# Gathers of the second cross attention: ten at a group's beginning, six behind its first three items

## The reference, cut to what matters

```python
x = x + L0_ffn(layernorm(x))      # 64 experts, 8 of them per row
x = x + L1_xattn(layernorm(x), ctx_1024)
...
# end of L0_ffn: eight expert outputs of a row, weighted and added
slot_out = yb[dest] * topk_w
out = zeros(T, h).at[slot_token].add(slot_out)
...
# L1_xattn: 16 heads of 128; queries and keys are RMS-normalized over the head
q = rmsnorm(q, gq); k = rmsnorm(k, gk)
attn = softmax(einsum('bqhd,bkhd->bhqk', q, k) / sqrt(128))
out = einsum('bhqk,bkhd->bqhd', attn, v) @ Wo
```

## Time and profile before

| | |
|---|---|
| runs | 2551.67, 2556.38, 2558.78 us; median 2556.38 |
| profiled execution | 2556.95 us, span 2554.9 us |
| PE busy | 2466.8 us, 97% of the span |
| DVE, ACT, POOL busy | 1304.8, 1310.7, 753.5 us |
| mean granted TensorE clock | 0.989 of full speed |
| second cross attention in the span | from about 1258 to about 1883 us |

### The profile page before, as it was taken

How to read it: one execution, slowest core, us unless ns; L and a number is a source line. 1 busy time by engine, 2 the same in 40 slices (tenths; PEclk the granted TensorE clock), 3 DMA queues, 4 the chain that set the end, 5 groups by cost and what they waited for, 6 DMA issues and landing times. The chain is left out here.

```text
span 2554.9 us, 61096 instructions
## 1 busy us (share of the span) xinstructions
PE 2466.8 (97%) x19044; PEld 1873.8 (73%) x19044; DVE 1304.8 (51%) x4749; ACT 1310.7 (51%) x4901; POOL 753.5 (29%) x897
## 2 busy tenths in 40 slices
PE   8999999999999999999889999999989999999988
PEld 6888888877644444544567887788878888888877
DVE  4555555556577764444455444555434444444434
ACT  3555555554366666666576556666623333333342
POOL 1222222337546540001443333331151111111032
PEclk9999999999899999999999999999999999999999
DMA  6222222110140004441454444442372000000033
GB/s 208 65 66 66 66 66 66 57 56 1 47 165 13 1 18 120 125 122 42 102 158 118 114 117 111 125 124 88 88 178 89 8 8 8 8 8 7 10 96 122
DMA packets 176868, 195.20 MB, mean 76 GB/s; under 512 B 40074, under 2 KB 142536, under 8 KB 175971
## 3 DMA queue, kind: packets, MB, share of 16 engines
q1 hardware_dynamic: 153074, 157.81, 21.2%
q0 software_dynamic: 17744, 32.60, 5.6%
q10 hardware_dynamic: 5920, 3.28, 0.7%
HBM read 150.44 MB, written 56.62 MB: 81 GB/s over the span
## 5 line engine op out<-in xcount | busy, mean ns | idle before, releaser
L299 PE MATMUL rt_kn_key_ps<-moe_w_wk,all_big 128*128 128x512 f32 x560 | 250.2, 600 | 0.8 <-DVE moe_kn_stats L348 0.4
L858 ACT ACTIVATE xa_probsT<-xa_probsT_ps 128x256 f32<-128x256 f32 x512 | 190.8, 374 | 97.6 <-PE xa_probsT_ps L692 90.7
L2449 PEld LDWEIGHTS sa_work_ps<-sa_xnT,all_big 128*128 128x128 f32 x2048 | 230.0, 192 | 9.6 <-issue 6.2
L2449 PE MATMUL sa_work_ps<-sa_xnT,all_big 128*128 128x128 f32 x2048 | 233.5, 276 | 2.8 <-POOL all_big L2304 2.3
L715 PE MATMUL xa_misc_ps<-cross_folded,xa_mixT 128*128 128x256 f32 x1024 | 230.1, 380 | 0.0
L715 PEld LDWEIGHTS xa_misc_ps<-cross_folded,xa_mixT 128*128 128x128 f32 x1024 | 194.1, 190 | 28.9 <-issue 2.9
L692 PE MATMUL xa_probsT_ps<-all_ident,xa_probs 128*128 128x128 f32 x1024 | 197.4, 275 | 7.4 <-DVE xa_probs L999 6.7
L999 DVE TENSOR_SCALAR xa_probs<-xa_probs,xa_share 128x257 f32<-128x257 f32 x512 | 187.3, 387 | 14.3 <-DVE xa_share L997 0.5
L299 PEld LDWEIGHTS rt_kn_key_ps<-moe_w_wk,all_big 128*128 128x128 f32 x560 | 104.8, 192 | 120.6 <-issue 114.5
L850 ACT ACTIVATE xa_probs<-xa_probs,xa_shift,xa_row_scale 128x257 f32<-128x257 f32 x256 | 152.6, 596 | 78.7 <-DVE xa_shift L983 78.4
L320 ACT ACTIVATE rt_kn_key_ps<-rt_kn_key_ps 128x128 f32<-128x128 f32 x560 | 148.4, 265 | 85.0 <-PE rt_kn_key_ps L299 85.0
(11 more groups left out here) (402 smaller groups left out, 5022.5 us busy)
## 6 DMA issues: line engine op xcount, KB each, us to landing
all_big<-rk SPq DMA_DIRECT2D x256, 128.5 KB
xa_pair<-pairs SPq DMA_DIRECT2D x64, 256.5 KB, 14.5
pairs<-all_big SPq DMA_DIRECT2D x64, 128.5 KB, 3.1
moe_w_wk<-in_ctx_dram SPq DMA_DIRECT2D x64, 128.0 KB, 2.5
pairs<-xa_keys SPq DMA_DIRECT2D x64, 128.0 KB, 2.1
cross_folded<-in_L_ffn_w_gate_dram SPq DMA_DIRECT2D x32, 192.0 KB, 2.6
cross_folded<-in_L_ffn_w_up_dram SPq DMA_DIRECT2D x32, 192.0 KB, 2.8
ff_rows<-pairs SPq DMA_DIRECT2D x35, 128.0 KB, 2.1
```

The source lines that it names most:

```text
L299: pe.matmul(self.key_ps[m % self.banks][0:n, :], self.ctxT[:, c * P:c * P + n], self.wk[:, q * 512:(q + 1) * 512], start=True, stop=True). ...
L858: act.activation(probsT[:, b % 2, :, r * P:(r + 1) * P], probsT_ps[s % 2][:, 0:KB * P].rearrange("p (k n) -> p k n", k=KB), ACT.Copy).then ...
L2449: ins = pe.matmul(ps[:, j, :], w[:, c, h * HD:(h + 1) * HD], xnT[:, c, :], start=(c == 0), stop=(c == NC - 1))
```

## The change

`FRONT` is NB // 2 + 1 = 5. At b = 0 POOL now issues the gathers 0 to 9 in one go, and behind each of the first three mixed items (b = 1, 2, 3) two more, 10 to 15. Behind b = 4 to 7 it waits for nothing and gathers nothing. `norm_scale` keeps its place at b = 5, and the wait for all gathers keeps its place behind the list. Rows, counts and data of the gathers are the same.

```diff
         PORTION = G * K0 // NB
+        FRONT = NB // 2 + 1
...
                     if more and b == 0:
                         next_places(i + 2)
-                    if more:
-                        if b:
-                            pool.wait_ge(mixed, i * NB + (RING + b))
-                            apart(pool, pool_passed)
-                        gather(range(b * PORTION, (b + 1) * PORTION))
+                    if more and b == 0:
+                        gather(range(FRONT * PORTION))
+                    elif more and b <= NB - FRONT:
+                        pool.wait_ge(mixed, i * NB + (RING + b))
+                        apart(pool, pool_passed)
+                        gather(range((FRONT + b - 1) * PORTION, (FRONT + b) * PORTION))
```

## The result

The changed kernel takes 2585.07 us (median of four, 2582.83 to 2587.14) against 2556.47 us for the kernel before on the same chip: ratio 1.0114, 95% interval [1.0097, 1.0132], 29 us slower. The forecast was no change. The profiled span grew from 2554.9 to 2580.7 us, by 25.8.

The account below looks back on a forecast made before the run. PE was taken as the bound, busy 97% of the span, with gathers touching only seven stalls. Terms -2.4 + 1.5 + 1.3 = +0.4 us on the profiled execution gave a median of 2556.8 us, no change; range 2550.5 to 2562.

Parts of the forecast that it names:

- What bounds the kernel, and which load is late: Second cross attention, groups 0 to 5: PE waits for `weigh`, DVE 10.4 us for key scales; item 7's scales are late.
- Groups 1 to 5, what the front costs: Start of each group: front gathers delay item 4's keys and so item 5's scales; 0.3 us per group, 1.5 us.
- the price that it took for a gather in a burst: Delay of loads per front gather, from windows before group 0 with loads at about 108 GB/s: 0.29 us.
- six gathers: Groups 1 to 5: the front gathers that start behind 1669 and push item 4's keys from 1678.2 to about 1679.9.
- 1.5 us of gap: Groups 1 to 5, loads before item 5's scales: a fixed part of some 1.5 us that can cover delay, called plausible.
- relief of 0.5 us: Groups 1 to 5: item 7's scales land 0.5 us earlier with two gathers less ahead, 0.25 us each.
- the clock: PE's granted clock falling behind long stalls: no term in the forecast sum; about 1.6 us in the rival with slower loads.
- Groups 1 to 5, the gain: Item 7's scales, with the pair of b = 4 moved ahead: 0.5 us in four groups, 0.4 in group 2; 2.4 us.
- Group 0: First group's items: five more gathers ahead of item 7's scales at 0.25 us each, a cost of 1.3 us.
- Edits that cost nothing: `norm_scale` and the waits for gathers before `row_scales` and `take`: these move or shrink, but PE waits for neither.
- The front pushes the scales: slower: Rival, groups 0 to 5: at 0.84 us a gather the front delays scales by 13.5 us in all, 2569.9 us; chance 0.07.
- middle case: Within the slower rival: loads get half, 0.65 us a gather, sum +8.7 us, 2565.1 us; 0.03 of that rival's chance.

Follow-up runs that it names:

- no_front_eight: Against the kernel before: the eight gathers that the change put at the front left out of each group, pairs of b = 0 to 3 kept; ratio 0.9975.
- front_tiny: The changed kernel with each of the ten front gathers cut to 16 rows; ratio to the kernel before 1.0117, repeated 1.0131.
- the paced kernel: Ten front gathers, the last six each behind an idle POOL operation, the other six behind items 5 to 7; 0.9971 and 0.9979 of the kernel before.

## Why the prediction was wrong, point by point

**What bounds the kernel, and which load is late.** Right for the kernel before, and as far as it goes: PE's stalls come from `weigh`, and that from scales. After the change the waits begin with item 5 or 6, not 7.

**Groups 1 to 5, what the front costs: this step failed**, in the price that it took for a gather in a burst. It was 0.29 us, "from the eight that go out back to back before group 0". Two things were wrong with it. The reading: it took the rate at which POOL issues, 101 GB/s, for what gathers moved. By the packet records they moved 64 GB/s of these 8 us and the loads 145, not 108, so these windows show no loss of the loads at all; the gathers fell behind instead (issued from 1260.0 to 1269.3, moved from 1262.0 to 1274.6). And the place: in the groups, item 4's scales met a pile of gathers, and loads and gathers shared evenly, 62 to 66 GB/s beside 60 to 62.

What the runs showed in its place is a price of 0.7 to 0.9 us a gather. PE's idle time in the five stages grew by 10.4 us. The prediction's sum, with six gathers and 1.5 us of gap, gives 5 * (6p - 1.5 - 0.5) = 10.4 for p = 0.68, with its relief of 0.5 us kept, and 5 * (6p - 1.5 - 2p) = 10.4 for p = 0.90, with the relief at the same price. Count and gap were not measured by themselves. The second term that failed is the clock, which the forecast had at nothing: its four falls are 6.8 us of the 17.6.

**Groups 1 to 5, the gain** (-2.4 us). No run has this pair alone. no_front_eight, which leaves it out with the six behind it, gained 0.25% [0.07%, 0.42%], some 6.5 us. A gain of the forecast size is consistent with that and is not shown by itself; the loss covered it.

**Group 0** (+1.3 us). Measured +9.9: 6.5 of waiting, and some 3.6 from the clock, of which the fall that began at 1287.2 has 2.2. There item 5's scales met the burst, too (first to last packet 1302.2 to 1319.4), and DVE waited for them. The prediction saw that items 5 and 6 would be hit and argued that their stalls "lie within that of item 7"; instead item 5's alone was 10.78 us, where no wait for scales before was over 2.2.

**Edits that cost nothing.** Held: POOL's and DVE's waits for gathers shrank (17.6 to 5.6, 6.3 to 3.9 us) and PE's list has neither.

**The rivals.** "The front pushes the scales: slower" had mechanism and place right, was given 0.07, and its 2569.9 us was still 15 us short. Its price of 0.84 was of the right size. Short were group 0, where it had 4.2 us and 6.5 were waited, and the clock, for which it had 1.6 us where the falls behind stalls cost some 8. Its middle case was that loads and gathers take turns of like size and loads get half, 70 of 139 GB/s. The trace of the changed kernel bears that out while item 4's scales move: 62 to 66 GB/s for the loads and 60 to 62 for the gathers. The Trainium skill's rule for that case ("DMA: Bandwidth & Descriptors", section "Queues, rings and completion order") has each DMA engine take its queues in turn, packet by packet. In those 12 to 13 us 184 to 196 gather packets and 247 to 298 packets of loads moved, so the trace agrees in the rough with turns, with more than one packet of the loads to one of the gathers; the 3.2 to 3.5 us ahead of the loads' first packet stand in no case. The prediction's remark that beside 101 GB/s of gathers the loads still had 108 rests on the wrong reading above. The rule spoke against the change, in the right direction, and the price from the wrong windows outvoted it.

**What stood in no case**: that ten issues in a row hold up signals between the engines. It does not appear in the first pair of traces, and a chip of the other kind loses the same 1% in large part by it. Why the two kinds lose so nearly alike is not shown. It may be chance: while the engines stand still the loads can catch up.

**Open** are: why a gather's packet takes up to twice as long in a group's dense row, even with no load beside it (0.48 to 0.58 us, against 0.30 by twos); how much of the changed kernel's loss on chips A is the front alone; what holds up the signals; whether chips A have that at all under another load (front_tiny did not meet one); and where the paced kernel's gain over the kernel before comes from.

## What to carry to other kernels

Give indirect gathers a distance that the DMA engines can keep up with, measured in the place where they will run: here one per 3 us beside loads was free, and ten at one per 1.3 us cost 0.7 to 0.9 us each with six more close behind. Moving ten transfers "to where there is room" lost without pauses and won with them, the other six standing at the group's end both times. Do not take the rate of issue for the rate of moving: look at the packets. Take a price for contention from a window in which the same two streams meet, and where there is none, let the range hold the case that the other stream gets next to nothing. When a cut of bytes or rows changes nothing, count the issues, and look for waits whose signal comes long after the work.

## What the runs showed of the hardware

- A gather's cost goes with rows and density: 0.08 us of packet time a row in pairs, 0.16 to 0.2 in a group's dense row, the same for rows of 512 bytes and of 1 KB. DMA engines can be busy at a share of 1.00 and move 93 GB/s.
- Gathers of 128 rows of 1 KB, issued every 1.30 us with no load beside them, moved at 79 to 84 GB/s, one in about 1.6 us. Beside them the loads of another queue got 62 to 66 GB/s in place of 112 to 119.
- While POOL issued seven to sixteen indirect transfers in a row, and for up to some 3 us behind, one kind of chip had gaps of 4 to 15 us without a recorded signal of PE, ACT or DVE, even at a DMA share of 0.2. Four in a row did nothing.
- A POOL operation of 1.67 us that computes nothing of use, in front of six gathers in each group, made the same kernel 0.9% to 1.1% faster on chips B; against one of 0.22 us it made it 0.5% faster on chip A.
